# An attention and expert block on one core: the expert products of a step regrouped from four places into two

## The reference

```python
sa, ca, ga, sb, cb, gb = split(silu(c) @ wmod)          # per batch; ga, gb kept at |.| >= 0.25
h = layernorm(x) * (1 + ca) + sa
q, k, v = split(h @ Wqkv + bqkv)                          # 16 heads of 8
dist2 = |k_i|^2 + |q_j|^2 - 2 k_i.q_j
x = x + ga * ((exp(-dist2 * sigma) @ v) @ Wproj + bproj)
h = layernorm(x) * (1 + cb) + sb
mask = top 2 of 8 of softmax(h @ w_router.T + b_router)   # 0 or 1, no weights
x = x + gb * sum_e mask_e * (h @ w_experts[e].T + b_experts[e])
```

## Time and profile before

| | |
|---|---|
| median of 3 runs | 229.1 us (227.3 to 229.19) |
| the profiled execution | 230.45 us |
| its span, first to last instruction | 228.4 us |
| around the span | 2.05 us |
| first scores of step 3 | 51.88 us after the span's start |
| first scores of step 15 | 198.31 us |
| mean granted TensorE clock | 0.977 of 2.4 GHz |

### The profile page before, as it was taken

The page is one execution under the profiler, slowest core; times in us unless marked ns, Lnnn a source line. Parts: engine busy times, 40 slices in busy tenths (PEclk is TensorE's granted clock), DMA queues, the critical chain, the costliest instruction groups (busy, mean ns, idle before and its releaser), DMA issues.

```text
span 228.4 us, 8135 instructions
## 1 busy us (share of the span) xinstructions
PE 211.7 (93%) x3230; PEld 149.2 (65%) x3230; DVE 166.0 (73%) x589; ACT 169.8 (74%) x254; POOL 141.9 (62%) x207
## 2 busy tenths in 40 slices
PE   7788987999999999999999999999899999999780
PEld 6464544576777776767767776776676767676580
DVE  6894536277877778777868687878678777868685
ACT  3217888888888888878787988888788878767160
POOL 6725564565858585857677595858385856305465
PEclk9967999999999999999999999999999999999996
DMA  6462323231434342432325133424342323300001
GB/s 164 128 199 83 132 78 120 87 118 61 152 75 146 90 147 90 143 89 93 123 76 164 61 119 98 139 69 153 80 145 70 141 69 104 108 1 26 23 3 46
DMA packets 22471, 22.93 MB, mean 100 GB/s; under 512 B 2330, under 2 KB 20258, under 8 KB 22434
## 3 DMA queue, kind: packets, MB, share of 16 engines
q1 hardware_dynamic: 21962, 21.79, 29.6%
q10 hardware_dynamic: 472, 0.62, 0.8%
HBM read 6.65 MB, written 2.12 MB: 38 GB/s over the span
## 4 chain that ended last, share of the span: by engine, by line
PE 73%; POOL 5%; DMA 5%; ACT 5%; DVE 4%; SPq 4%; issue 3%; POOLq 0%; DVEq 0%
PE att_ps L911 22%; PE scores L893 10%; PE ffn_ps L1025 7%; PE qkv_ps L926 7%; DMA st<-norm_parts 5%; PE ffn_ps L1026 5%; PE ffn_ps L1027 5%; PE mid_ps L969 2%; ACT probs L490 2%; PE qkv_ps L956 2%; PE qkv_ps L935 2%; PE mid_ps L1002 2%; POOL hl L406 2%; SPq L316 2%; PE scores L840 2%
## 5 line engine op out<-in xcount | busy, mean ns | idle before, releaser
L490 ACT ACTIVATE probs<-scores 128x1024 f32<-128x1024 f32 x128 | 124.0, 1022 | 20.6 <-PE scores L893 20.6
L911 PE MATMUL att_ps<-probs,vpad 128*32 128x256 f32 x1024 | 68.5, 385 | 0.0
L682 DVE SCALAR_TENSOR_TENSOR acc<-ffn_ps,mask,acc 128x128 f32<-128x128 f32 x218 | 61.3, 343 | 9.6 <-PE ffn_ps L1027 9.5
L893 PE MATMUL scores<-st 32*128 32x256 f32 x512 | 37.3, 331 | 4.3 <-DMA st<-norm_parts 2.6
L911 PEld LDWEIGHTS att_ps<-probs,vpad 128*32 128x32 f32 x1024 | 26.7, 109 | 19.6
L361 POOL TENSOR_TENSOR ve<-stats,eps 128x2 f32<-128x2 f32 x32 | 6.2, 195 | 51.5 <-DVE stats L662 51.5
L1025 PE MATMUL ffn_ps<-we_hi,h_hi 128*128 128x256 f32 x110 | 35.7, 325 | 0.6 <-POOL h_lo L423 0.6
L893 PEld LDWEIGHTS scores<-st 32*128 32x128 f32 x512 | 23.5, 185 | 13.1 <-issue 3.3
L1026 PE MATMUL ffn_ps<-we_hi,h_lo 128*128 128x256 f32 x110 | 30.7, 279 | 0.0
L1027 PE MATMUL ffn_ps<-we_lo,h_hi 128*128 128x256 f32 x110 | 30.6, 278 | 0.0
L404 POOL TENSOR_TENSOR sq<-qkf 128x512 f32<-128x512 f32 x15 | 15.6, 1042 | 19.6 <-DVE qkf L688 19.6
(11 more groups left out here) (146 smaller groups left out, 332.2 us busy)
## 6 DMA issues: line engine op xcount, KB each, us to landing
st<-hl SPq DMA_DIRECT2D x47, 256.0 KB
rb_all<-rb_rows SPq DMA_DIRECT2D x16, 192.0 KB, 3.4
out_dram<-x_all SPq DMA_DIRECT2D x16, 128.0 KB, 3.1
x_all<-in_L_attn_x_dram SPq DMA_DIRECT2D x13, 128.0 KB, 3.3
st<-norm_parts SPq DMA_DIRECT2D x60, 16.0 KB
we_sb<-in_L_ffn_w_experts_dram SPq DMA_DIRECT2D x1, 512.0 KB, 5.3
w_mod_sb<-in_L_wmod_dram SPq DMA_DIRECT2D x1, 256.0 KB, 4.4
st<-hl ACTq DMA_DIRECT2D x1, 256.0 KB
```

Source lines behind the costliest of these rows:

```text
L490: nc.scalar.activation(probs[:, g, 2 * half:2 * half + 2, :], scores[:, 2 * half:2 * half + 2, :], ACT.Exp, scale=two_sigma).then_inc((exp ...
L682: v.scalar_tensor_tensor(acc[:, q, t, :], y, m, acc[:, q, t, :], ALU.mult, ALU.add).then_inc(acc_step, 1)
L893: i = pe.matmul(scores[:, r, t * T:(t + 1) * T], st[rows, par, g, t * P:(t + 1) * P], st[rows, par, g, T:2 * T], start=True, stop=True)
L911: i = pe.matmul(att_ps[r * ROWS:(r + 1) * ROWS, 0:T], heads[:, g * ROWS:(g + 1) * ROWS], probs[:, g, r, t * T:(t + 1) * T], start=(g == 0 ...
```

## The change

On TensorE a step now has the chunks in pairs. Chunks 2 and 3 of batch k-3 stand together after the scores of group 1; chunks 0 and 1 of batch k-2 stand together at the step's end, with `turn_x2` and `turn_x` between them. `turn_mask` stands after the scores of group 2, and `expert_bias` just ahead of those of group 3. The products of `pv` are moved later by three half groups: at the step's start come the second half of group 2 and all of group 3 of batch k-1, with the router of batch k-2 between them, and in the step itself only groups 0, 1 and half of 2. The router, the choice of experts and the splitting of `h2` of a batch thus move one step later. `fill(4)`, four products of 128 columns in step 0 whose result nobody reads, is gone.

The two chunks of a pair use two banks: `qkv_ps` and `ffn_ps` for 0 and 1, `att_ps` and `ffn_ps` for 2 and 3. New waits follow: chunk 0 waits for VectorE's `values(k+1)`, chunk 1 for chunk 3 of the batch before, chunk 2 for `o_ok`, `pv` of group 0 for chunk 2, `qk_rows` for chunk 0. `turn_x` writes to the second half of `mid_ps` from batch 2 on.

`high_parts` and `mask_rows` move from ScalarE to VectorE (but for batch 0 and the last step). GpSimd's norm for `turn_x` comes after its work for queries and keys. The transfers are the same. The last step has an order of its own, and the tail is the old one with `experts(13, 3)` a little later.

The high parts (703), the other layer norm's statistics, the mask's copy (744) and the split of `h2` (749, 751) now stand ahead of `values` (720), and one chunk stands behind it. The diff, cut to its core:

```diff
@@ -244,13 +244,18 @@
         def f_bank(b, c):
+            if b <= NB - 4:
+                return (qkv_ps, ffn_ps, att_ps if b < NB - 4 else qkv_ps, ffn_ps)[c][:, :]
             if b == NB - 3:
                 return (qkv_ps, ffn_ps)[c % 2][:, :]
             if b == NB - 2:
                 return (qkv_ps[:, :], scores[:, 0, :], scores[:, 1, :], scores[:, 3, :])[c]
-            if b == NB - 1:
-                return (ffn_ps[:, :], att_ps[:, :], qkv_ps[:, :], scores[:, 0, :])[c]
-            return ffn_ps[:, :]
+            return (ffn_ps[:, :], att_ps[:, :], qkv_ps[:, :], scores[:, 0, :])[c]
+        def x_bank(b):
+            return qkv_ps[:, 0:T] if b < 2 else mid_ps[:, T:2 * T]
         def v_bank(b):
...
                 i.then_inc(wqk_ok, 1)
-            def high_parts(b):
-                act.wait_ge(qkf_ok, b + 1)
-                if b > 0:
-
-                    act.wait_ge(st_in[(b - 1) % 2], stacked(b - 1))
+            def high_parts():
+                act.wait_ge(qkf_ok, 1)
                 nc.scalar.copy(hl[:, 0:4:2, :], qkf[:, :, :]).then_inc(hi_ok, 1)
...
                     act.wait_ge(ld_be, 32)
                     nc.scalar.copy(be_hi[:, :], be_sb[:, :]).then_inc(be_hi_ok, 1)
-                if has(k + 1) and k >= 0:
-                    high_parts(k + 1)
-                if has(k - 2):
-                    start_acc(k - 2)
                 if has(k):
                     exp(k, 1, 0)
                     exp(k, 1, 1)
                 if has(k + 1) and k >= 0:
                     norm_high(k + 1)
+                if last:
+                    mask_rows(k - 2)
                 if has(k):
                     exp(k, 2, 0)
+                if last:
+                    start_acc(k - 2)
+                if has(k):
                     exp(k, 2, 1)
-                if has(k - 1):
+                if has(k - 2) and not last:
+                    start_acc(k - 2)
+                if last:
                     second_norm(k - 1)
                 if has(k):
                     exp(k, 3, 0)
@@ -548,8 +554,10 @@
                     act.wait_ge(xt_ps, k + 3)
                     if k == -2:
                         act.wait_ge(mod_sb, 2)
-                    nc.scalar.activation(h1[:, :], qkv_ps[:, 0:T], ACT.Identity, bias=shift_col[:, 0, k + 2:k + 3],
+                    nc.scalar.activation(h1[:, :], x_bank(k + 2), ACT.Identity, bias=shift_col[:, 0, k + 2:k + 3],
                                          scale=scale_col[:, 0, k + 2:k + 3]).then_inc(h1_ok, 1)
+                if has(k - 1) and not last:
+                    second_norm(k - 1)
             def tail():
...
                                 bqk_col[:, :].unsqueeze(2).broadcast_to([P, 2, T]), ALU.add).then_inc(qkf_ok, 1)
+            def high_parts(b):
+                dve.wait_ge(st_in[(b - 1) % 2], stacked(b - 1))
+                dve.wait_ge(qkf_ok, b + 1)
+                v.tensor_copy(hl[:, 0:4:2, :], qkf[:, :, :]).then_inc(hi_ok, 1)
             def norm_rows(b):
                 dve.wait_ge(n_ps, b + 1)
...
+            def first_stats(b):
+                if b <= 2:
+                    dve.wait_ge((ld_x, ld_x0, ld_x1)[b], 16)
+                elif b >= 4:
+                    dve.wait_ge(ld_xb[b % 2], 16 * (b // 2 - 1))
+                ln_stats(0, b, b % 2, bn1)
             def step(k):
+                last = k == NB - 1
                 if has(k - 3):
...
+                    experts(k - 3, 1)
+                if k < 0:
+                    first_stats(k + 2)
                 if k == -2:
                     silu()
                     first_normalise()
                     modulation(0)
                 if k == -1:
                     bias_columns()
...
+                if k == -1:
                     queries_keys(k + 1)
                 if k == -1:
                     first_parts()
...
                     norm_rows(0)
...
+                    values(0)
                     modulation(1)
                     gate_rows()
                     expert_weights(0)
                     queries_keys(1)
                     expert_weights(1)
+                    return
+                if k == -2:
+                    return
+                if has(k - 2):
+                    choose(k - 2)
+                if has(k + 1):
+                    if k > 0:
+                        queries_keys(k + 1)
+                    high_parts(k + 1)
+                if has(k - 3):
+                    experts(k - 3, 2)
+                if has(k - 1):
+                    first_residual(k - 1)
+                if has(k + 1):
+                    norm_rows(k + 1)
+                if has(k - 1):
+                    second_stats(k - 1)
+                if has(k + 2):
+                    first_stats(k + 2)
+                if has(k - 2) and not last:
+                    mask_rows(k - 2)
+                if has(k - 1):
+                    normalise(k - 1)
+                if has(k - 2):
+                    split_h2(k - 2)
+                if has(k + 1):
+                    values(k + 1)
+                if has(k - 3):
+                    experts(k - 3, 3)
                 if k == 0:
                     split_weights()
                 if has(k - 2):
...
+                    experts(k - 2, 0)
+                if last:
+                    experts(k - 2, 1)
                     split_h2(k - 1)
...
                     choose(k - 1)
+                    experts(k - 2, 2)
             def tail():
                 b = NB - 1
                 experts(b - 2, 3)
                 first_residual(b)
+                second_stats(b)
                 experts(b - 1, 0)
...
                         if b > 0:
                             pe.wait_ge(o_ok, b)
+                            if 3 <= b < NB - 1:
+                                pe.wait_ge(acc_step, STEPS * (b - 3) + 3 * EC * NT)
                         else:
                             pe.wait_ge(wr_sb_ok, 1)
...
                 pe.wait_ge(h1_ok, b + 1)
+                if b >= 4:
+                    pe.wait_ge(acc_step, STEPS * (b - 4) + EC * NT)
+                elif b >= 2:
+                    pe.wait_ge(v_ok, b)
                 if b == 0:
...
-                for t in range(NT):
-                    i = pe.transpose(qkv_ps[:, t * P:(t + 1) * P], xn[:, b % 2, t * C:(t + 1) * C], ident[:, :])
+                elif b > 3:
+                    pe.wait_ge(acc_init, b - 3)
+                for t in range(NT):
...
                         pe.wait_ge(we_ok, 1)
-                if b == NB - 3 and c == 0:
-                    pe.wait_ge(v_ok, NB)
-                elif b == NB - 3:
-                    pe.wait_ge(acc_step, steps(b, (c - 1) * EC * NT))
+                if b <= NB - 4 and c == 0:
+                    pe.wait_ge(v_ok, b + 4)
+                elif b <= NB - 4 and c == 2 and b < NB - 4:
+                    pe.wait_ge(o_ok, b + 3)
+                elif b <= NB - 4 and c == 1:
+                    if b > 0:
+                        pe.wait_ge(acc_step, steps(b, 0))
+                elif b <= NB - 3:
+                    pe.wait_ge(acc_step, steps(b, 0 if c == 0 else (c - 1) * EC * NT) if c < 2 else steps(b, (c - 1) * EC * NT))
                 elif b == NB - 2 and c == 0:
                     pe.wait_ge(acc_step, steps(b - 1, 3 * EC * NT))
                 elif b == NB - 1 and c != 1:
                     pe.wait_ge(acc_step, (steps(b - 2, STEPS), 0, steps(b - 1, EC * NT), steps(b - 1, 2 * EC * NT))[c])
-                elif b < NB - 2 and NC * b + c > 0:
-                    pe.wait_ge(acc_step, EC * NT * (NC * b + c))
                 for t in range(NT):
...
                 if k == -1:
                     start()
                     return
...
+                if k == -2:
+                    turn_x(0)
+                    warm_up(1)
+                    return
+                last = k == NB - 1
+                qk_scores(k, 0)
+                if has(k - 1):
+                    pv(k - 1, 2, (1,))
+                if has(k - 2):
+                    router(k - 2)
                 if has(k - 1):
                     pv(k - 1, 3)
...
+                if has(k + 1):
                     qk_rows(k + 1)
...
+                qk_scores(k, 1)
                 if has(k - 3):
+                    experts(k - 3, 2)
                     experts(k - 3, 3)
...
                 if has(k - 1):
                     project(k - 1)
...
+                if has(k + 1):
                     norms(k + 1)
+                if last:
+                    pv(k, 0)
+                    turn_mask(k - 2)
+                qk_scores(k, 2)
+                if last:
+                    expert_bias(k - 2)
+                if has(k - 2) and not last:
+                    turn_mask(k - 2)
+                if not last:
+                    pv(k, 0)
+                if has(k + 1):
+                    values(k + 1)
+                pv(k, 1)
+                if last:
+                    experts(k - 2, 0)
```

(14 more changed lines are left out.)

85 lines of the change are left out of this document (16 added, 69 removed).

## The result

The changed kernel takes **238.25 us** (median of 4, 236.34 to 241.22) against 229.14 for the kernel before beside it: ratio 1.04, 95% interval 1.0333 to 1.0467. It is slower by 9.1 us, where the forecast said 4.4. The same pair on the chip of a later group gave 1.0311 (1.0251 to 1.0371). The profiled executions differ by 7.5 us of span (235.9 against 228.4), and the profile of before had come out 1.35 above its own median.

What follows compares the result with a forecast made beforehand. TensorE was taken to set the middle's pace, the stacking transfers as second bound. Head +0.6, middle +1.8 and end +2.0 gave +4.4 on the median 229.1, so 233.5 us (own range 230.5 to 236; with rivals 226 to 239).

Steps and rivals of the forecast that it cites:

- The product floor: TensorE in a middle step: fewer changes of array shape save 0.2 us, floor 11.9 instead of 12.1; as rival 0.20.
- written-out starts: TensorE's new step listed by start times, from pv 2 at 0.44 to the next step at 11.9 us.
- VectorE: VectorE's queue in a middle step: values out at 9.9, chunk 0 at 9.8, no room left; step 12.0, other end 12.4.
- Square first: the cast waits up to 1.0: Stack term's case where GpSimd's square precedes VectorE's cast: cast waits up to 1.0 us, low parts come 0.2 later.
- The fourth: Rival: VectorE or the port lock sets the pace, values late by 0.4 or more, steps 12.4 to 12.5, 237 us; 0.15.
- The stack: Stacking transfers ahead of a step's first scores: last issue at 9.6 to 9.8, ordinary landing 11.5 to 11.7, hidden under 12.0.
- late landings: Stacking transfers in steps 3 to 14: four of 12 land at 12.3 us, two at 13.5, beyond the ordinary 12.0.
- +1.8 for the middle: Steps 3 to 14: 6 x 12.0 + 4 x 12.3 + 2 x 13.5 = 148.2 against 146.4; ends -2.5 and +5.4.
- The head: Steps before step 3: fillers gone, but high parts queue on VectorE and step 2 waits; +0.6 us, from -1.2 to +1.5.
- The end: From step 15's first scores: one step more of delay to empty; +2.0 us, between 1.35 (TensorE) and 3.0 (VectorE).

Runs made afterwards that it cites:

- a_psum: The changed kernel with the high parts made on VectorE from PSUM with the bias added, not copied from SBUF: 232.45 us, ratio 1.016 to before.
- b_psum: The kernel before with the high parts moved from ScalarE to VectorE and made from PSUM: 228.31 us, ratio 1.006 to before.
- a_end: The changed kernel with only VectorE's and GpSimd's work at the end reordered, the cast left as it is: 235.49 us, ratio 1.029 to before.

## Why the prediction was wrong

- **The product floor** was forecast as 11.9 and is 12.00 (a_psum): the regrouping gains 0.1 us per step, not 0.2. Its written-out starts hold to 0.1 up to scores 2 (forecast 5.65, in the trace 134.16 - 128.46 = 5.70). The change to scores 1 takes 130.34 to 131.32, 0.98, hence 0.12 as read. The 0.1 is lost at the mask's turn: a_psum takes 0.49 from scores 2 to it and 0.24 on to the `pv`, 0.73 where the forecast had 0.65.
- **VectorE: the step that failed.** The forecast had the cast of the high parts at 0.42 us and so the residual at "about 5.6" into the step, held only by the projection: VectorE's own queue would have been free at about 5.1. In the trace the residual starts at 134.51 - 128.46 = 6.05, because the cast takes 1.30 beside the square, and of the 0.88 more 0.45 come through. The forecast had priced this for the stack ("Square first: the cast waits up to 1.0") and not carried it into VectorE's own queue, where chunk 2 and the residual stand behind. And it did not name who waits for the residual: the change gave the mask's turn a wait for `x1_ok`, and TensorE's queue stands behind it. For an ordinary step the forecast took 12.0 us, which is what a_psum measures without the collision; the wait adds 0.41 to each.
- **The rival that came nearest.** The fourth, with 12.4 to 12.5 us a step and 237 us, had been given 0.15. It named the port lock and came out in the number, but partly by luck: its condition was that the values are late, and they were out 0.6 us before chunk 0.
- **What held the cast up.** The Trainium skill (SBUF — State Buffer, SBUF: two separate sides) says that whichever of the two engines comes first gets the shared pair of ports for a whole instruction while the other fully blocks. The trace agrees in the main: 1.30 against 0.41, with the square 20 ns ahead; the cast ends 0.28 after the square, a little sooner than a full 0.41 behind it. By the same section this holds for a VectorE operation in a two-port mode or with two SBUF inputs. The addition of a_psum and b_psum, with one input in PSUM and one in SBUF, has not two SBUF inputs, and its 0.68 beside a square agrees.
- **The stack.** Last issue forecast at 9.6 to 9.8 into the step, in the trace 138.29 - 128.46 = 9.83. But of steps 3 to 14 late landings lengthened one and not six, by 1.2 us where the forecast's sum has 4 x 0.3 + 2 x 1.5 = 4.2. As the steps themselves became 12.4, the landings had more cover; in a_psum, with 12.00, they lengthen two, by 0.9 in all. So the forecast's +1.8 for the middle had the right sign for the wrong reason: without the collision the middle is 144.8, 1.6 us shorter than before.
- **The head** was forecast +0.6 and measured +0.8, inside its scatter, so it neither supports nor counters the term.
- **The end** was forecast +2.0, with 3.0 as the upper bound, and measured +3.0. So it met its upper bound by the wrong sum. The added work alone costs less than the forecast's lowest figure of 1.35, as a_end shows: +0.7 without the waits. What was not followed is the order, which costs the other 2.3: chunk 3 of batch 12 stands behind a normalise that waits 1.08 for its rstd, and TensorE waits 1.52 for that chunk; the last rstd stands behind a gating on GpSimd, and TensorE waits 1.11 for the rows normalised with it.

```profile
210.03 0.60 DVE L738 TENSOR_SCALAR x2n<-x_all,stats,rstd 128x128 f32<-128x128 f32 x2 [1.08 <-POOL rstd L368]
...
211.21 1.12 DVE L690 SCALAR_TENSOR_TENSOR acc<-ffn_ps,mask,acc 128x128 f32<-128x128 f32 x4
...
212.47 0.36 PE L1080 MATMUL qkv_ps<-we_hi,h_hi 128*128 128x256 f32 x1 [1.52 <-DVE acc L690]
```

So of 7.5 us in the traces (forecast 4.4), the cast's collision takes 12 x 0.41 = 4.9, the two waits at the end 2.4, the deeper end 0.7, the head 0.8; the shorter floor gives back 1.2. These come to 7.6.

## What to carry to other kernels

Before a copy is moved to VectorE, look at what GpSimd does at that very moment on operands in SBUF: here a cast of 0.42 us became as long as GpSimd's instruction and 0.3 more, but not where the value was made from PSUM or the two started at different times. A cost found at one place must be carried through the whole queue of its engine, to the first instruction of another engine that waits there. And where a pipeline gets deeper, write out the last step's queues in order, on GpSimd too: an edit that moves one item ahead of a wait gained only once every item that was needed sooner had moved with it.
